# Mixer of an adaLN block: z products put beside the silu pass, silu of z read from PSUM, and a new order of steps

## What is computed

```python
h = _layernorm(x) * (1 + ca) + sa;  xn = layernorm(h, ln_w, ln_b)
zxbcdt = xn @ in_proj_w                      # 256 -> 512 (z) + 768 (xBC) + 32 (dt)
dt = jax.nn.softplus(dt + dt_bias)
xBC = jax.nn.silu(causal_conv1d(xBC, conv_w, conv_b))       # 4 taps; x_ssm 512, Bm 128, Cm 128
y = ssd_scan(xh, dt, Bm, Cm, A) + D_skip * xh               # 32 heads of 16, state of 128
y = y * jax.nn.silu(z)
y = y * rsqrt(mean(y * y) + 1e-05) * rms_w;  out = y @ out_proj_w + h
```

## Time and profile before

| | |
|---|---|
| median of 3 runs | 3193.36 us (3186.01 to 3193.88) |
| profiled execution, own time | 3180.88 us |
| its span, first to last instruction | 3179.2 us |
| PE busy over the span | 2799.2 us (88%) |
| DVE busy | 1839.9 us (58%) |
| ACT busy | 1384.6 us (44%) |
| POOL busy | 678.1 us (21%) |
| mean granted TensorE clock | 0.943 |

### The profile page before, as it was taken

One profiled execution on the slowest core, in us unless ns is written; L12 is line 12 of the kernel. 1 busy time (PEld: TensorE's weight loads), 2 busy tenths in 40 slices (PEclk: granted clock), 3 DMA queues, 4 the chain that ended last, 5 costly groups with the idle time before them and its releaser, 6 DMA issues. The chain is left out here.

```text
span 3179.2 us, 46142 instructions
## 1 busy us (share of the span) xinstructions
PE 2799.2 (88%) x16998; PEld 2086.3 (66%) x16998; DVE 1839.9 (58%) x3504; ACT 1384.6 (44%) x2394; POOL 678.1 (21%) x716
## 2 busy tenths in 40 slices
PE   0488888888888888869999799999999999999999
PEld 0354555455555555458888687887878787878787
DVE  4688888888888888746767433333333333333332
ACT  0566666666666666536555322222222222222221
POOL 5022222222222222210000122222222222222221
PEclk6799989998999899879999899999999999999999
DMA  3010101010101010035211100000000000000000
GB/s 125 29 35 20 35 20 35 20 35 20 35 21 35 21 35 11 28 104 208 70 62 64 48 13 7 11 14 16 14 16 14 16 14 16 14 16 14 16 14 8
DMA packets 104858, 107.06 MB, mean 34 GB/s; under 512 B 35897, under 2 KB 98617, under 8 KB 102977
## 3 DMA queue, kind: packets, MB, share of 16 engines
q1 hardware_dynamic: 99520, 103.81, 10.1%
q10 hardware_dynamic: 5120, 0.19, 0.1%
HBM read 71.41 MB, written 40.94 MB: 35 GB/s over the span
## 5 line engine op out<-in xcount | busy, mean ns | idle before, releaser
L1597 PE MATMUL fbank<-hid,fw 128*128 128x512 f32 x4096 | 962.3, 395 | 0.0
L1597 PEld LDWEIGHTS fbank<-hid,fw 128*128 128x128 f32 x4096 | 766.1, 187 | 187.0
L1747 DVE TENSOR_TENSOR hid<-fhf,hid 128x512 fp32r<-128x512 f32 x384 | 264.9, 690 | 704.3 <-POOL hid L1704 704.3
L1704 POOL TENSOR_SCALAR hid<-fhf 128x512 fp32r<-128x512 f32 x384 | 271.1, 706 | 1040.2 <-ACT fhf L1676 760.8
L808 ACT ACTIVATE mh<-ebank 128x512 f32<-128x512 f32 x512 | 302.0, 598 | 415.0 <-PE ebank L663 413.8
L1121 DVE SCALAR_TENSOR_TENSOR mh<-mh,gm 128x512 f32<-128x512 f32 x512 | 403.2, 794 | 1.8 <-ACT mh L808 1.8
L663 PE MATMUL ebank<-cright,cleft 102*128 102x512 bf16 x512 | 211.1, 413 | 64.1 <-ACT cin L847 28.9
L1676 ACT ACTIVATE fhf<-fbank,sh2c 128x512 f32<-128x512 f32 x128 | 88.0, 688 | 382.4 <-PE fbank L1597 382.4
L676 PE MATMUL yin<-mh,xpad 128*32 128x128 f32 x4096 | 230.5, 300 | 27.1 <-DVE mh L1121 26.6
L650 PE MATMUL ebank<-ah,win 128*128 128x512 f32 x640 | 246.7, 425 | 7.1 <-ACT cin L847 6.6
L1676 ACT ACTIVATE fhf<-fbank,sh1c 128x512 f32<-128x512 f32 x128 | 88.1, 688 | 320.8 <-PE fbank L1597 320.6
(11 more groups left out here) (180 smaller groups left out, 4380.1 us busy)
## 6 DMA issues: line engine op xcount, KB each, us to landing
fx<-x_d SPq DMA_DIRECT2D x17, 512.0 KB, 3.9
xs<-in_x SPq DMA_DIRECT2D x16, 512.0 KB, 4.3
h_d<-in_h SPq DMA_DIRECT2D x16, 512.0 KB, 5.4
o_d<-o SPq DMA_DIRECT2D x16, 512.0 KB, 2.9
mo<-o_d SPq DMA_DIRECT2D x16, 512.0 KB, 3.8
mx<-in_x SPq DMA_DIRECT2D x16, 512.0 KB, 4.8
x_d<-mx SPq DMA_DIRECT2D x16, 512.0 KB, 2.8
fw<-h_d SPq DMA_DIRECT2D x2, 4096.0 KB, 15.2
```

Source lines behind the costliest of these rows:

```text
L1597: mm = pe.matmul(bank[banks.slot(key)][:], w[:, k, m * P:(m + 1) * P].bitcast(dt), h[:, k, :].bitcast(dt), start=(k + n == 0), stop=(k == ...
L1704: pool.tensor_scalar(hid[i % 2][0][:, m, :], hf[j % 3][:], 1.0, 0.0, ALU.mult, ALU.add)\
L1747: dve.tensor_tensor(hid[i % 2][1][:, m, :], hf[j % 3][:], hid[i % 2][0][:, m, :].bitcast(F32), ALU.subtract).then_inc(c_lo.sem, 1)
```

## The change

No instruction of arithmetic is added. Four ACT copies (`keep_z`) and one silu over 2048 columns of SBUF go away; in their place ACT takes four silus of 512 columns straight from PSUM, after the silu of xc. PE's four z products move from n = 17, 19, 21, 23 to n = 27, all four in one step, the same in which ACT has its silu pass (26 before). POOL's first gating of a block waits for the last of these silus instead of the silu of xc. Almost every other position is set anew:

| step | engine | before | after |
|---|---|---|---|
| skip term dx of chunk c, steps after 8c | ACT | 11 | 8 |
| ec, ysq | ACT | 10, 16 | 9, 15 |
| addends | DVE | 9 | 10 |
| new_state | DVE | 8 | 11 |
| to_state | PE | 10 | 12 |
| x_by_token: product, reader | PE, DVE | -3, -5 | -4, -4 |
| mean square, residual | DVE | 14, 15 | 15, 16 |
| gating, rms power | POOL | 10, 14 | 5, 10 |
| affine (n) | ACT | 1, 2 | 0, 1 |
| dt product, chain from (n) | PE, DVE | 3, 1 | 4, 3 |
| convolution products (n) | PE | 5, 7, 9, 11, 13, 15 | 4, 8, 11, 12, 13, 16 |
| their evacuations (n) | ACT | 6, 8, 10, 12, 14, 16 | 5, 8, 10, 12, 13, 16 |
| taps from (n) | DVE | 4 | 5 |
| layer norm parts (n) | DVE | 17, 20, 21, 22 | 19, 22, 23, 25 |

```diff
-AFFINE_AT = (1, 2)
+AFFINE_AT = (0, 1)
-WV_AT = 12
-DTW_AT = 19
-DTW_READ_AT = 20
-Z_AT = (17, 19, 21, 23)
-Z_EVAC_AT = (18, 20, 22, 24)
-SILU_AT = 26
-TAIL_AT = 22
-LN_AT = (17, 20, 21, 22)
-LN_POW_AT = (18, 24)
-LN_NORM_AT = (23, 30)
+WV_AT = 15
+DTW_AT = 20
+DTW_READ_AT = 18
+SILU_AT = 27
+TAIL_AT = 28
+LN_AT = (19, 22, 23, 25)
+LN_POW_AT = (15, 20)
+LN_NORM_AT = (24, 30)
...
+def chunk_at(S, at):
+
+    q, i = divmod(S - at, NG)
+    return q if i == 0 and has_chunk(q) else -1
...
-            if n in Z_AT:
-                yield ("in", j, Z_AT.index(n))
+            if n == SILU_AT:
+                for m in range(QI):
+                    yield ("in", j, m)
...
-                    if n in Z_AT:
-                        in_proj(j, Z_AT.index(n))
+                    if n == SILU_AT:
+                        for m in range(QI):
+                            in_proj(j, m)
...
-            def keep_z(j, m):
-                key = ("in", j, m)
-                made(act, key)
-                if m == 0 and j >= 2:
-                    act.wait_ge(c_yg.sem, c_yg.at(0, NC * (j - 1)))
-                nc.scalar.activation(sz[j % 2][:, m, :], tile(key)[:], ACT.Copy).then_inc(free(key), 1)
-
             def gates(j):
-                released(act, ("in", j, QI - 1))
-                nc.scalar.activation(sz[j % 2][:], sz[j % 2][:], ACT.Silu)
                 act.wait_ge(c_conv.sem, c_conv.at(0, XM * (j + 1)))
                 nc.scalar.activation(xc[j % 2][:], xc[j % 2][:], ACT.Silu).then_inc(c_xc.sem, 1)
+                if j >= 2:
+                    act.wait_ge(c_yg.sem, c_yg.at(0, NC * (j - 1)))
+                for m in range(QI):
+                    key = ("in", j, m)
+                    made(act, key)
+                    nc.scalar.activation(sz[j % 2][:, m, :], tile(key)[:], ACT.Silu).then_inc(free(key), 1)
...
                 if q % NC == 0:
-                    pool.wait_ge(c_xc.sem, c_xc.at(0, q // NC + 1))
+                    released(pool, ("in", q // NC, QI - 1))
                 pool.tensor_tensor(yg[:], yg[:], sz[q // NC % 2][:, :, tokens(q)], ALU.mult).then_inc(c_yg.sem, 1)
```

More of the change, by code:

```diff
@@ L133 @@
 FIRST = -SPAN
-LAST = (CHUNKS + 1) * NG + 1
+LAST = (CHUNKS + 2) * NG + 1
+OP_AT = 16
+YOFF_AT = 9
+ST_AT = 12
+XT_AT = -4
+BT_AT = -2
+YSQ_AT = 15
+EC_AT = 9
+SKIP_AT = 8
+BCOPY_AT = -1
+GATED_AT = 5
+RMS_AT = 10
+STATE_AT = 11
+ADD_AT = 10
+XREAD_AT = -4
+GM_AT = -4
+MEAN_AT = 15
+RES_AT = 16
 NT_AT = (0, 1)
-AFFINE_AT = (1, 2)
+AFFINE_AT = (0, 1)
 AL_AT = (0, 1)
-DT_AT = 3
+DT_AT = 4
 SOFTPLUS_AT = 4
-CHAIN_FROM = 1
+CHAIN_FROM = 3
 CHAIN_PER = 2
 CHAIN = SERIES + 13
-CONV_AT = (5, 7, 9, 11, 13, 15)
-EVAC_AT = (6, 8, 10, 12, 14, 16)
-TAPS_FROM = 4
+CONV_AT = (4, 8, 11, 12, 13, 16)
+EVAC_AT = (5, 8, 10, 12, 13, 16)
+TAPS_FROM = 5
 WEXP_AT = 15
-WV_AT = 12
-DTW_AT = 19
-DTW_READ_AT = 20
-Z_AT = (17, 19, 21, 23)
-Z_EVAC_AT = (18, 20, 22, 24)
-SILU_AT = 26
-TAIL_AT = 22
-LN_AT = (17, 20, 21, 22)
-LN_POW_AT = (18, 24)
-LN_NORM_AT = (23, 30)
+WV_AT = 15
[6 more added lines that the diff above has]
+LN_NORM_AT = (24, 30)
 def has_off(q):
@@ L180, in act_bank_order @@
             yield ("eb", q, i)
-        if i == 1 and has_off(q - 1):
-            yield ("ec", q - 1)
+        c = chunk_at(S, YOFF_AT)
+        if has_off(c):
+            yield ("ec", c)
         if j < BLOCKS:
@@ L191, in act_bank_order @@
                 yield ("dtw", j)
-            if n in Z_AT:
-                yield ("in", j, Z_AT.index(n))
-        if i == 6 and has_chunk(q + 1):
-            yield ("bT", q + 1)
+            if n == SILU_AT:
+                for m in range(QI):
+                    yield ("in", j, m)
+        c = chunk_at(S, BT_AT)
+        if c >= 0:
+            yield ("bT", c)
 def dve_bank_order():
     for S in range(FIRST, LAST):
[L201 to L212, removed]
+        c = chunk_at(S, OP_AT)
+        if c >= 0:
+            yield ("op", c)
+        c = chunk_at(S, YOFF_AT)
+        if has_off(c):
+            yield ("yoff", c)
+        c = chunk_at(S, ST_AT)
+        if has_state(c):
+            yield ("st", c)
+        c = chunk_at(S, XT_AT)
+        if c >= 0:
+            yield ("xT", c)
+        c = chunk_at(S, BT_AT)
+        if c >= 0:
+            yield ("bt", c)
 FFN_SHAPES = ((KD, FF), (KD, FF), (KF, FF), (KF, FF), (KF, D))
@@ L727, in b_by_token @@
                 x_ = xc[q // NC % 2]
+                if q % NC == 0:
+                    pe.wait_ge(c_xc.sem, c_xc.at(0, q // NC + 1))
                 key = ("bt", q)
@@ L778, in _ @@
                     intra(*divmod(S - LAG, NG))
[L779 to L789, removed]
+                c = chunk_at(S, OP_AT)
+                if c >= 0:
+                    project(c)
+                c = chunk_at(S, YOFF_AT)
+                if has_off(c):
+                    state_decay(c)
+                    from_state(c)
+                c = chunk_at(S, ST_AT)
+                if has_state(c):
+                    to_state(c)
+                c = chunk_at(S, XT_AT)
+                if c >= 0:
+                    x_by_token(c)
+                c = chunk_at(S, BT_AT)
+                if c >= 0:
+                    b_by_token(c)
                 if j < BLOCKS:
@@ L914, in _ @@
                     exponent(q, i)
[L915 to L922, removed]
+                c = chunk_at(S, YSQ_AT)
+                if c >= 0:
+                    y_out(c)
+                c = chunk_at(S, EC_AT)
+                if has_off(c):
+                    state_decay(c)
+                c = chunk_at(S, SKIP_AT)
+                if c >= 0:
+                    skip(c)
+                c = chunk_at(S, BCOPY_AT)
+                if c >= 0:
+                    b_by_token(c)
                 if j < BLOCKS:
@@ L933, in _ @@
                         weights_by_token(j)
-                    if n in Z_EVAC_AT:
-                        keep_z(j, Z_EVAC_AT.index(n))
                     if n == SILU_AT:
@@ L973, in _ @@
                     power(2 * (j + 1) + LN_POW_AT.index(n) + 1)
[L974 to L977, removed]
+                c = chunk_at(S, GATED_AT)
+                if c >= 0:
+                    gated(c)
+                c = chunk_at(S, RMS_AT)
+                if c >= 0:
+                    rms_power(c)
         @block.vector
@@ L1175, in _ @@
                     masked(q, i)
[L1176 to L1187, removed]
+                c = chunk_at(S, STATE_AT)
+                if has_state(c):
+                    new_state(c)
+                c = chunk_at(S, ADD_AT)
+                if c >= 0:
+                    addends(c)
+                c = chunk_at(S, XREAD_AT)
+                if c >= 0:
+                    x_by_token(c)
+                c = chunk_at(S, GM_AT)
+                if c >= 0:
+                    b_by_token(c)
+                c = chunk_at(S, MEAN_AT)
+                if c >= 0:
+                    square_mean(c)
+                c = chunk_at(S, RES_AT)
+                if c >= 0:
+                    residual(c)
                 if j < BLOCKS:
```

## The result

The changed kernel takes 3040.65 us (median of 4 runs, 3029.34 to 3044.58) against 3193.19 us: a ratio of 0.952, with a 95% interval of 0.949 to 0.955. The profiled execution has a span of 3037.6 us against 3179.2, so 141.6 us less.

A forecast was written before the change was run, and what follows sets the result against it. DVE was taken as the bound, idle 12.1 us a period. A period of 71.0 us instead of 78.3, times 14, gave 102 us, plus 4 at the ends: 3193.4 - 106 = 3087 us, range 3038 to 3152.

The forecast's parts named there:

- The sum: Whole kernel: a period of 71.0 us instead of 78.3, times 14 is 102 us, with the ends 106 us.
- the ends: First period and stretch after the last silu: the same waits in part, 4 us gained, bounds 0 and 8.
- What bounds the kernel: Mixer: DVE is the bound outside one stretch at the silu pass; it is idle for 12.1 us of a period.
- PE's 61.4 us at full clock: PE's work in a period without the low clock's 4.9 us, shorter than DVE's 66.2 us.
- ACT's arithmetic: Silu pass on ACT: 1.7 us a period saved, worth nothing by itself; 7.9 us between exponents instead of 7.2.
- DVE in the hold: While ACT gives no exponents: DVE has 11.6 us of work against 9.7, doesn't wait, and the 3.85 us dx wait goes.
- Leads: Producers' lead over DVE: mean square and state waits of 2.3 and 1.6 us shrink; 0.5 us of both kept.
- The restart: After the silu pass: `low` waits for `affine` on ACT, 3.0 us a period for two waits, bounds 0 and 3.85.
- the rival: Low clock moves to n = 18 to 26, z products at 1.2 GHz: 75 us a period, 3147 us; chance 0.20.
- My signs: Profile after: clock at 1.00 over whole periods, DVE busy 66 us of 71, dx wait almost nowhere, PSUM silus 0.60 to 0.69 us.
- The slower rival: Silu pass meets a DVE without work in hand: 79.5 us a period, 17 us more in all, 3210 us; chance 0.08.
- The rival of no effect: DVE's waits are replaced one for one, as by the mask waiting for exponents: 3184 to 3203 us; chance 0.04.

The follow-up runs named there:

- g_taps_cut_after: The changed kernel without one of three convolution taps on DVE (six instructions a block): 2986 us, ratio 0.938.
- f_restart_back: The changed kernel with affine back at n = 1, 2, the dt product at 3 and DVE's chain from 1: 3096 us, ratio 0.971.
- a_z_alone: The kernel before, old order, with only the z part: four z products in the silu pass step, silus from PSUM: 3275 us, ratio 1.026.
- e_dx_back: The changed kernel with the skip term dx on ACT back at 11 steps after the chunk's start: 3105 us, ratio 0.975.
- c_dx_alone: The kernel before with only the skip term dx on ACT moved, from 11 to 8 steps after the chunk's start: 3141 us, ratio 0.987.
- d_chunk_steps: The kernel before with all positions within a chunk from the new order, positions within a block and z part unchanged: 3174 us, ratio 0.996.

## Why the prediction was right, and where it was not

3087 us with a range of 3038 to 3152 was forecast, 3041 us came, under 3 us inside the low end. The sum had 106 us, the profiled execution shows 141.6: 125.5 in the 14 periods (forecast 102) and 16 at the ends (forecast 4). The mechanism was right in the main, dx and the leads above all; the size was a quarter too small.

**What bounds the kernel.** The first step was wrong for the kernel before. I read busy shares of 97 and 98% as DVE setting the pace outside one stretch. Taking 4 us from it there gave 0.2%. What was gained in the long stretch was waited for behind it, for the state product and for dx. For the changed kernel, to which the sum was applied, the reading holds: 3.4 of 4.0 us. PE's 61.4 us at full clock was right too: in g_taps_cut_after, with 0.5 us a period at 1.2 GHz, PE is busy for 61.3 (858.83 in 14).

**ACT's arithmetic.** Right. The silu from PSUM takes 590 ns, the lower of my two bounds. I had ACT wait at most 0.5 us for the fourth product; it is 0.79. The hold is 8.2 us, forecast 7.9.

The drain that the Trainium skill adds to a table load (ScalarE: Activation LUTs, What ACT_TABLE_LOAD costs) is not in this trace either: 613.49 + 1.28 is 614.77, and the silu starts at 614.78.

**DVE in the hold.** Right in that no mask waits for an exponent there (1.2 us in 14 periods). In the pass shown ACT came later than I allowed, 3.3 us after the last tap (610.2 to 613.49) and not 1.2, and DVE had more to do, 12.4 us from there to the end of the mask of step 28 without its waits, against 11.6. The wait of the addends for PE's group, 1.4 us a period, was not in the sum. I had named the four products as PE's work, and not who waits for what they push back. The same wait was 1.2 us a period before; I put it among the smaller ones, though it was longer than that for POOL's power, and then at nothing.

**Leads.** Right: 3.9 us a period of waits for mean square and state went to zero, where I kept 0.5.

**The restart.** The mechanism was right and its size was not: 3.0 us forecast, 0.6 measured. The 2.4 us wait is not why, for it makes ACT late as well, and `low` waits about 0.6 us in every period, also where the addends wait for nothing. In the pass of 823.07 (T = 821.14) ACT has the first `affine` done at T + 17.2 (forecast 17.5), and DVE comes to it at T + 17.7 (forecast 16.7). So the first wait is gone, and the second is 0.5 us where I had up to 1.5. The 1.0 us is about what the state multiply has more with POOL's gating beside it (1.77 us at 830.62 against 0.69). f_restart_back shows that the place matters: with the old positions the two waits are 4.3 us.

**The sum.** Busy 65.5 + 1.4 + 0.9 + 0.6 + 0.3 is 68.7 of 69.4 us, against 66.2 + 4.8. The two wrong terms, the restart and the addends, are -2.4 and +1.4; DVE's busy time (-0.7) and the leads (-0.5) make most of the rest. The ends had the same waits as the periods, as I said, but in full: 12.9 us in the last stretch alone.

**The rivals.** The low clock did move to n = 19 to 26, as the rival had it, but for 4.9 us a period and not over the z products. Its price was still the largest wait that is left, by the table of the passes: the addends' 1.4 us a period, where the rival had 4.0 in all. My signs had the clock at 1.00 over whole periods; 11 of the 14 have a stretch at 1.2 GHz. The forecast's reading that the clock would stay up is thus wrong for most periods. The slower rival's mechanism is real: in a_z_alone the hold meets a DVE with under two steps in hand, and costs 89 us. The order is what keeps the change from that, and dx is one part of it: with dx put back (e_dx_back) the kernel is still at 3105. The rival of no effect is refuted.

## What to carry to other kernels

A wait once in a period (here for a step that stands behind another engine's long pass) can swallow a saving made between two such waits, on whichever engine: here 4 us taken off DVE and 4 off PE gave nothing, alone or together. An engine at 97% busy on either side of it need not be the bound. Move what the others wait for ahead of the pass first, and only then fill the pass with work of a third engine, for filled first it cost time here. When an engine gets a block of work in one place, list what it pushes back in its own queue and who waits for that, and the bank ring that it shifts.

## What the runs showed of the hardware

The same DVE instruction took 0.23 us in one order and 1.31 in another, or 0.69 and 1.5 on average. The order alone moved DVE's busy time from 65.3 (c_dx_alone) to 68.2 us a period (d_chunk_steps) with the same instructions. The rows of two groups by line, in the kernel before and in d_chunk_steps (count, busy us, mean ns, idle before):

```profile
L1164 DVE TENSOR_TENSOR state<-state,dec 128x512 f32<-128x512 f32 x43 | 29.5, 686 | 22.7 <-PE bank L713 22.7
...
L1029 DVE TENSOR_SCALAR dden<-dabs 128x128 f32<-128x128 f32 x14 | 18.3, 1306 | 0.0
```

```profile
L1205 DVE TENSOR_TENSOR state<-state,dec 128x512 f32<-128x512 f32 x42 | 62.1, 1478 | 0.0
...
L1070 DVE TENSOR_SCALAR dden<-dabs 128x128 f32<-128x128 f32 x14 | 3.2, 227 | 27.7 <-ACT dabs L871 27.7
```

In the changed kernel the state multiply at 622.23 takes 1.76 us with POOL's gating at 621.85 beside it. I had counted this price for masks alone, and as the same in every order. That POOL is the cause is read from the timeline; no run took POOL's work away.

Work taken off PE can lengthen the time at 1.2 GHz: with 4 us a period less of z products it rose from 13.2 to 22.2 us in the kernel before and from 4.9 to 8.5 in the changed one. Not every PE instruction takes twice as long there. In the changed kernel's stretch from 605.1 to 611.9 us the eight matmuls of L733 took 2.02 us instead of 1.11 (629.20), and that of L690 0.59 instead of 0.38.
